# Four graph layers on one core: shorter factor chains in layer 1's preparation, and layer 3's normalisation, weights, products and first row of sums in one block

## Chip, cores and metric

One core of a Trainium2 chip runs the whole program in one launch. The metric is the device time in microseconds (us), and less is better. TensorE is PE in the profile, VectorE is DVE, ScalarE is ACT, GpSimd is POOL, SyncE (which issues most DMAs) is SP.

## What is computed

A node matrix x (3327 x 256, float32) passes four layers that share one 0/1 adjacency (about 1% ones, with a diagonal). Each layer takes h = relu(layernorm(x)) and adds its result to x:

```python
h = jnp.maximum(_layernorm(x), 0.0); x = x + L0(h)   # 8-head graph attention
h = jnp.maximum(_layernorm(x), 0.0); x = x + L1(h)   # cosine attention
h = jnp.maximum(_layernorm(x), 0.0); x = x + L2(h)   # 8-head hard attention (argmax)
h = jnp.maximum(_layernorm(x), 0.0); x = x + L3(h)   # mean over neighbours

# L1:  Wh = h @ W.T;  sim = Wh @ Wh.T / (|Wh| |Wh|.T + EPS);  softmax(masked sim) @ Wh
# L3:  agg = mask @ h / max(deg, 1)
#      out = relu(concat([h @ W_self + b_self, agg @ W_nb + b_nb]) @ W_comb + b_comb)
```

## The kernel before

The nodes are 26 tiles of 128; x stays in SBUF as `k.X`. The layers are separate, with a barrier of all engines between blocks and layers. Within a block each engine has its own list of instructions, written out by hand and taken strictly in order, and semaphores are the only link between the lists. Every float32 operand of a product is split into a float16 high part and a float16 rest; a product is three matmuls per half of the 256 features (`hi_lo_products`), so 6 matmuls of 256 columns per tile.

**Layer 1's preparation** (`cosine_prepare`, L980) handles tiles in four portions (0 to 3, 4 to 11, 12 to 19, 20 to 25) and seven quads of four tiles (the last has two). DVE measures mean and variance (`measure`, L1076, then `gather`, L1081) and finds from them, with a square root on ACT (`root`, L1198) and one Newton step, each tile's factor and shift (`factors`, seven small DVE instructions, L1092 to L1104, each waiting for the one before). POOL applies them (`shifted`, L1035, tile by tile), PE turns the quad by transposes (`turn`, L1278), ACT takes relu and the high part (`high`, L1204), DVE the rest (`low`, L1111). PE multiplies by the weights (`project`, L1292), ACT stores the product Wf and its squared norms (`take`, L1209, L1215), POOL casts (`cast`, L1040) and DVE takes the rest (`rest`, L1117). From the norms in four portions DVE finds 1/|Wh| (`norms`, L1125 to L1138, seven small instructions with a root on ACT, L1221), POOL scales the rows (`unit`, L1047), PE turns them (`unit_turn`, L1309), ACT and DVE split them (`unit_high` L1232, `unit_low` L1144). `row` writes the reciprocal norms to DRAM. The order of each list is written at its end: POOL's runs from `shifted(0)` over `cast(0)`, `shifted(3)`, `shifted(4)`, `cast(1)`, `shifted(5)`, `shifted(6)`, `unit(0)`, `unit(1)`, `cast(2)` on. The attention block `cosine_attend` starts after a barrier.

**Layer 3** has two blocks. The first is `normalise` (L71) with `mean_weights` (L2235) hooked into it: ACT applies factor, shift and relu tile by tile (L190), PE turns quads (L228), ACT and DVE split into `hT` (L196, L168); two halves, 0 to 7 and 8 to 25. The hooked part loads W_self, W_nb, W_comb and the biases, waits for all the loads together, transposes the weights (L2287), multiplies each with W_comb (L2294) and finds the joint bias (L2302, L2280), so that one product per source is left. The second block, `mean_aggregate`, loads the adjacency (two tile rows per transfer) and computes, for all 26 tiles, P = hT @ m, stored as high part and rest side by side (512 columns, L2371, L2406, L2417); then for each of 26 rows of tiles the sum of 26 matmuls of 512 columns (`sums`, L2385) and the row's own product (`own`, 6 matmuls, L2392). Row 0's sums are woven into the products:

```python
for jt in range(NT):
    if i == 0:
        if jt + LEAD < NT:
            neighbour(jt + LEAD)
        pe.wait_ge(s_pl, jt + 1)
```

ACT and DVE finish each row (L2411 to L2429) and SP stores it.

## Time and profile before

| | us |
|---|---|
| median of 3 runs (lowest to highest) | 2209.24 (2208.99 to 2215.06) |
| the profiled execution's own time | 2210.15 |
| its span | 2208.4 |

| engine | busy, us | share of the span |
|---|---|---|
| PE | 1979.8 | 90% |
| DVE | 1877.9 | 85% |
| ACT | 1607.4 | 73% |
| POOL | 914.7 | 41% |

The span goes from the first to the last instruction; 1.75 us of the execution's own time lie around it. The shares are averages over four layers with different limits, and each of the two places changed is a small part of the span. Layer 1's preparation runs from 672.2 to 736.3 us of the span, layer 3's first block from 1983.4 to 2019.3, its second from there to the end. A matmul's record is longer than its turn in the pipeline: back to back, the chain gives 0.216 us for one of 512 columns at full clock.

### The profile page before, as it was taken

To read this page: it belongs to the slowest core of one execution; us is meant where nothing else is said; L and a number is where in the kernel's file an instruction comes from. 1 tells how busy PE (TensorE), PEld (TensorE's weight loads), DVE (VectorE), ACT (ScalarE), POOL (GpSimd) and SP (SyncE) were. 2 spreads that over 40 slices of the span, in tenths; PEclk is the share of its full clock that TensorE was granted. 3 is DMA by queue.
4 is the path that set the end of the run, shared out by engine and by line. 5 is a ranking of instruction groups with operands and counts; after the bars stand their busy time and mean duration, and the time that the engine had idled before them with its cause. 6 is when DMAs were issued, how large, how long until landed. Compare 5 with 4: busy or idle time off the path is not lost. (4 is left out here: it accounts for less than half of the span.)

```text
span 2208.4 us, 58755 instructions
## 1 busy us (share of the span) xinstructions
PE 1979.8 (90%) x23674; PEld 1552.3 (70%) x23674; DVE 1877.9 (85%) x4155; ACT 1607.4 (73%) x1914; POOL 914.7 (41%) x952
## 2 busy tenths in 40 slices
PE   4748999999995899999887999999999999977999
PEld 4548999999994788888654666666666666655544
DVE  5587999999997899988668999999999999985222
ACT  4557999999994776552266999999999999885100
POOL 0020000000005434446316888888888888860000
PEclk9958999999998899999898999999999999997999
DMA  9798221221201156679564212222122211101222
GB/s 306 288 367 308 75 90 57 75 89 55 95 22 41 54 147 160 156 164 190 124 177 144 71 38 69 71 71 70 37 71 71 71 65 42 40 7 48 81 81 71
DMA packets 178078, 235.13 MB, mean 106 GB/s; under 512 B 112195, under 2 KB 143971, under 8 KB 174481
## 3 DMA queue, kind: packets, MB, share of 16 engines
q1 hardware_dynamic: 153408, 203.68, 30.1%
q10 hardware_dynamic: 24400, 27.70, 3.8%
q8 instruction: 188, 3.08, 0.6%
q14 instruction: 82, 0.67, 0.1%
HBM read 161.79 MB, written 49.00 MB: 95 GB/s over the span
## 5 line engine op out<-in xcount | busy, mean ns | idle before, releaser
L2200 DVE CUSTOM_DVE_ANT_0 h_S<-h_ps,off 128x832 f32<-128x832 f32 x832 | 800.1, 1019 | 17.4 <-PE h_ps L2099 16.3
L2099 PE MATMUL h_ps<-KS,QS 98*128 98x416 f16 x1664 | 441.5, 347 | 74.4 <-DVE h_mx L2200 43.0
L2159 ACT ACTIVATE h_H<-h_S,h_nmx 128x2048 fp8e4<-128x2048 f32 x208 | 416.7, 2003 | 69.7 <-DVE h_nmx L2206 69.7
L844 ACT ACTIVATE b_CA<-room,HC 128x1152 fp8e4<-128x1152 f32 (+1 forms) x384 | 435.5, 1219 | 0.0
L945 PE MATMUL b_pb<-xb,room 128*128 128x132 f16 x5408 | 415.8, 222 | 3.6 <-DVE room L906 3.2
L945 PEld LDWEIGHTS b_pb<-xb,room 128*128 128x128 fp8e4 x5408 | 341.9, 97 | 6.5 <-DVE room L906 6.0
L2053 POOL TENSOR_SCALAR h_gap<-h_S,h_nmx 128x1280 f32<-128x1280 f32 x208 | 277.1, 1332 | 91.2 <-DVE h_nmx L2206 81.6
L2058 POOL TENSOR_SCALAR h_H<-h_gap 128x1280 uint8<-128x1280 f32 x208 | 260.5, 1253 | 17.2
L926 PE MATMUL b_pz<-xb,adjT 128*128 128x134 f16 x2704 | 258.1, 222 | 4.3 <-PEq L306 4.3
L2130 PEld LDWEIGHTS h_po<-Vhl,h_HT 128*128 128x128 fp8e4 x5408 | 214.8, 98 | 64.9 <-ACT h_HT L2166 0.7
L2099 PEld LDWEIGHTS h_ps<-KS,QS 98*128 98x128 f16 x1664 | 95.8, 97 | 192.9 <-DVE h_mx L2200 119.0
L1422 POOL TENSOR_SCALAR c_MK<-c_ad 128x512 f16<-128x512 uint8 x169 | 155.1, 917 | 178.7 <-DVE c_V L1523 142.3
L1035 POOL TENSOR_SCALAR p_H<-X,p_sm 128x256 f32<-128x256 f32 x26 | 14.1, 556 | 515.9 <-DVE p_sm L1104 515.8
L2130 PE MATMUL h_po<-Vhl,h_HT 128*128 128x64 f16 x5408 | 225.9, 193 | 0.6 <-ACT h_HT L2168 0.6
L2166 ACT ACTIVATE h_HT<-h_pT 128x1024 uint16<-128x1024 uint16 x208 | 209.3, 1006 | 0.2 <-PE h_pT L2107 0.2
L859 DVE TENSOR_SCALAR b_CD<-room,HC 128x1152 uint8<-128x1152 f32 (+1 forms) x240 | 189.3, 789 | 0.8 <-PEq L306 0.8
L926 PEld LDWEIGHTS b_pz<-xb,adjT 128*128 128x128 fp8e4 x2704 | 184.5, 97 | 4.6 <-issue 4.6
L1579 PE MATMUL c_pa<-WHhi,c_V 128*128 128x257 f16 x676 | 185.6, 275 | 0.6 <-DVE c_V L1523 0.5
L1581 PE MATMUL c_pa<-WHhi,c_V 128*128 128x257 f16 x676 | 184.7, 273 | 0.0
L1580 PE MATMUL c_pa<-WHlo,c_V 128*128 128x256 f16 x676 | 183.9, 272 | 0.0
L906 DVE TENSOR_TENSOR room<-b_CA,adjT 128x288 int32<-128x288 int32 (+1 forms) x384 | 162.4, 442 | 16.0 <-ACT b_CA L844 15.8
L2385 PE MATMUL m_pa<-m_P,m_ad 128*128 128x512 f16 x676 | 154.3, 380 | 0.3 <-DVE m_P L2417 0.3
(246 smaller groups left out, 3192.0 us busy)
## 6 DMA issues: line engine op xcount, KB each, us to landing
h_rows<-in_adj_dram SPq DMA_DIRECT2D x24, 1663.5 KB, 7.4
room<-in_adj_dram SPq DMA_DIRECT2D x25, 832.0 KB, 6.6
room<-in_adj_dram SPq DMA_DIRECT2D x25, 831.5 KB, 7.5
e_dram<-c_U ACTq DMA_DIRECT2D x78, 256.0 KB, 3.1
xb<-xv_dram SPq DMA_DIRECT2D x44, 435.5 KB, 5.1
adjT_dram<-adjT SPq DMA_DIRECT2D x1, 10816.0 KB, 32.2
c_ad<-adjT_dram SPq DMA_DIRECT2D x13, 832.0 KB, 6.8
m_ad<-adjT_dram SPq DMA_DIRECT2D x13, 832.0 KB, 4.5
```

The source lines that it names most:

```text
L844: nc.scalar.activation(dst[:, 0:cols], elr[:, n % 2, 0:cols], ACT.Sigmoid, bias=HC[:, h, 1, jt:jt + 1], scale=STEP, saturate=False).then_i ...
L859: nc.vector.tensor_scalar(dst[:, 0:gn * P].bitcast(U8), elr[:, n % 2, 0:gn * P], HC[:, h, 0, jt:jt + 1], float(FP8_ONE), ALU.is_gt, ALU.mu ...
L926: last = nc.tensor.matmul(pz[:, z % 2, r * WZ:(r + 1) * WZ].rearrange("p (h d) -> p h d", h=2), k.adjT[:, g0 + 3 * b + r, jt, :], xb[:, m ...
L945: last = nc.tensor.matmul(pb[:, p, b, r * W:(r + 1) * W].rearrange("p (f d) -> p f d", f=2), B[:, u % RING_B, t * P:(t + 1) * P], xb[:, m ...
L1579: nc.tensor.matmul(pa[:, q, t, 0:D + 1], hi, WHhi[:, jt, :], start=first, stop=False, skip_group_check=True)
L2053: nc.gpsimd.tensor_scalar(gap[:], S[:, g % 2, CA:NP], nmx[:, g % 2:g % 2 + 1], -SHARPER, ALU.add, ALU.mult).then_inc(s_gap, 1)
L2058: nc.gpsimd.tensor_scalar(H[:, g % 2, CA:NP].bitcast(U8), gap[:], float(FP8_ONE), 0.0, ALU.min, ALU.max).then_inc(s_hB, 1)
L2099: last = nc.tensor.matmul(ps[:, ch % 2, b, 0:SB], QS[:, i % 2, h, :], KS[:, h, c0:c0 + SB], start=True, stop=True)
L2130: last = nc.tensor.matmul(po[:, i % 2, h * 2 * HD:(h + 1) * 2 * HD], wt[:, b, :, e], Vhl[:, b, e, h, :], start=(b == 0 and e == 0), stop=( ...
L2159: nc.scalar.activation(H[:, g % 2, 0:CA], S[:, g % 2, 0:CA], ACT.Exp, bias=nmx[:, g % 2:g % 2 + 1], scale=1.0, saturate=False).then_inc(s_ ...
L2166: nc.scalar.activation(HT[:, g % 2, 0:CA].bitcast(U16), pT[:, 0, :].bitcast(U16), ACT.Copy).then_inc(s_evA, 1)
L2200: nc.vector.tensor_tensor_reduce(out=two(S[:, g % 2, ch * SW:(ch + 1) * SW]), in0=ps[:, ch % 2, :, 0:SB], in1=two(off[:, i % 2, ch * SW:(c ...
```

## The change

**Layer 1's preparation.** The chain of `factors` has five instructions behind ACT's root in place of six, and `norms` five in all in place of seven (the constants move into scalar_tensor_tensor, and the factor 1e-8 moves into ACT's copy of `row`; the attention's logarithm reads the other array accordingly). ACT, not POOL, applies factor and shift to tiles 2, 3, 6, 7, 10 and 11. In DVE's and ACT's lists some entries trade places. In pieces:

```diff
+    COUNTED, NORMED = 7, 6
+    BY_ACT = (2, 3, 6, 7, 10, 11)
     NW = 3
     with ExitStack() as c:
...
             def unit(g):
                 for t in quad(g):
-                    pool.wait_ge(s_rsm, COUNTED * (norm_of(t) + 1))
+                    pool.wait_ge(s_rsm, NORMED * (norm_of(t) + 1))
...
                     elif n == 3:
-                        ins = nc.vector.tensor_tensor(b, a, ve, ALU.mult)
+                        ins = nc.vector.scalar_tensor_tensor(b, a, -0.5 * HSC, ve, ALU.mult, ALU.mult)
                     elif n == 4:
-                        ins = nc.vector.tensor_scalar(a, b, -0.5 * HSC, 1.5 * HSC, ALU.mult, ALU.add)
-                    elif n == 5:
-                        ins = nc.vector.tensor_tensor(rt, a, rs, ALU.mult)
+                        ins = nc.vector.scalar_tensor_tensor(rt, b, 1.5 * HSC, rs, ALU.add, ALU.mult)
                     else:
...
                 nc.vector.reciprocal(inv, root).then_inc(s_rsm, 1)
 
                 dve.wait_ge(s_rsm, at + 3)
-                nc.vector.tensor_tensor(e, inv, low2, ALU.mult).then_inc(s_rsm, 1)
+                nc.vector.tensor_tensor(e, inv, inv, ALU.mult).then_inc(s_rsm, 1)
                 dve.wait_ge(s_rsm, at + 4)
-                nc.vector.tensor_tensor(e, e, inv, ALU.mult).then_inc(s_rsm, 1)
+                nc.vector.scalar_tensor_tensor(e, e, -0.5, low2, ALU.mult, ALU.mult).then_inc(s_rsm, 1)
                 dve.wait_ge(s_rsm, at + 5)
-                nc.vector.tensor_scalar(e, e, -0.5, 1.5, ALU.mult, ALU.add).then_inc(s_rsm, 1)
-                dve.wait_ge(s_rsm, at + 6)
-                nc.vector.tensor_tensor(rcol[:, 0, t0:t1], e, inv, ALU.mult).then_inc(s_rsm, 1)
-                dve.wait_ge(s_rsm, at + 7)
-                nc.vector.tensor_scalar(rcol[:, 1, t0:t1], rcol[:, 0, t0:t1], NORM_EPS, None, ALU.mult).then_inc(s_rsm, 1)
+                nc.vector.scalar_tensor_tensor(rcol[:, t0:t1], e, 1.5, inv, ALU.add, ALU.mult).then_inc(s_rsm, 1)
 
             def unit_low(g):
...
-            measure(4, 6)
+            measure(4, 8)
             factors(0, 1, COUNTED - 1)
-            measure(6, 12)
+            measure(8, 12)
             gather(1)
             factors(1, 0, 1)
             factors(1, 1, COUNTED - 1)
+            measure(12, 14)
             low(0)
-            measure(12, 18)
-            low(1)
-            measure(18, 20)
+            measure(14, 20)
             gather(2)
             factors(2, 0, 1)
-            low(2)
+            low(1)
             factors(2, 1, COUNTED - 1)
             measure(20, NT)
             gather(3)
-            factors(3, 0, COUNTED - 1)
+            factors(3, 0, 1)
+            low(2)
+            factors(3, 1, COUNTED - 1)
             norms(0)
...
-            def take(g):
+            def shifted(t):
+                act.wait_ge(s_sm, COUNTED * (portion_of(t) + 1))
+                nc.scalar.activation(H[:, t, :], k.X[:, t, :], ACT.Identity, scale=rt[:, t:t + 1], bias=nb[:, t:t + 1]).then_inc(s_ha, 1)
+
+            def take(g, part=None):
                 for m in quad_pairs(g):
+                    if part is not None and m % 2:
+                        root(part)
...
             def row(part):
                 t0, t1 = NORM_PORTIONS[part]
                 act.wait_ge(s_row, part + 1)
-                nc.scalar.activation(rT[0:t1 - t0, part, :], pr[0:t1 - t0, 0:P], ACT.Copy).then_inc(s_rowc, 1)
+                nc.scalar.activation(rT[0:t1 - t0, part, :], pr[0:t1 - t0, 0:P], ACT.Copy, scale=NORM_EPS).then_inc(s_rowc, 1)
...
             root(0)
+            shifted(2)
+            shifted(3)
             act.wait_ge(s_wt, 1)
             nc.scalar.activation(w[:, 0], pr[:].rearrange("p (k n) -> p k n", k=KC), ACT.Copy, scale=WSC).then_inc(s_whi, 1)
             root(1)
             high(0)
+            for t in BY_ACT[2:]:
+                shifted(t)
             high(1)
+            root(2)
             take(0)
-            root(2)
             high(2)
-            take(1)
-            root(3)
+            take(1, part=3)
             norm_root(0)
             high(3)
...
         def _(pe):
             def turn(g):
-                pe.wait_ge(s_h, quad(g)[-1] + 1)
+                pe.wait_ge(s_h, sum(t not in BY_ACT for t in range(quad(g)[-1] + 1)))
+                if quad(g)[-1] in BY_ACT:
+                    pe.wait_ge(s_ha, BY_ACT.index(quad(g)[-1]) + 1)
                 for kc in range(KC):
...
-                pe.wait_ge(s_rsm, COUNTED * part + 7)
+                pe.wait_ge(s_rsm, NORMED * (part + 1))
...
+                                               scale=rcol[:, 2 * jp + j:2 * jp + j + 1])
                 ins.then_inc(s_ln, 1)
 
```

**Layer 3.** `normalise` and `mean_weights` give way to one function, `mean_prepare`, with the scheme of layer 1's preparation; `measure`, `gather`, `factors`, `low`, `root`, `high`, `shifted` and `turn` are as there. Its block also makes all the products P (two tiles at a time) and row 0's sums. The weights of the neighbours are loaded, turned and combined first, and each load has its own wait; the first two adjacency loads are issued in this block. `mean_aggregate` starts with `own(0)` and `sums(1)`; its tensors `Pn`, `pa` and `ad` are now made in `layer3`. The final loops over rows are unchanged.

```diff
+def mean_prepare(k, ap, hT, m, bias, ideg, Pn, pa, ad, s_in, s_first, adjT_dram):
...
+    SOURCES_IN = (1, 0)
...
+        @block.sync
+        def _(sp):
+            for s in SOURCES_IN:
+                sp.dma_start(raw[:, s], srcs[s][0].rearrange("(k p) c -> p k c", p=P)).then_inc(s_raw[s], 16)
+            sp.dma_start(comb[:].rearrange("p s k c -> p (s k) c"),
+                         ap["L3_gnn_W_comb"].rearrange("(k p) c -> p k c", p=P)).then_inc(s_comb, 16)
+            for s in range(2):
+                for kc in range(KC):
+                    sp.dma_start(bcol[:, s, kc:kc + 1], srcs[s][1][kc * P:(kc + 1) * P].rearrange("(p o) -> p o", o=1)).then_inc(s_small, 16)
+            sp.dma_start(bc[:], ap["L3_gnn_b_comb"].unsqueeze(0).to_broadcast([P, D])).then_inc(s_small, 16)
+            for q in range(2):
+                sp.dma_start(ad[:, q].rearrange("p t j i -> p t (j i)").bitcast(U8),
+                             adjT_dram[q * CT:(q + 1) * CT].rearrange("t p n -> p t n").bitcast(U8)).then_inc(s_in[q], 16)
...
+            for t in [t for t in range(NT) if t not in BY_ACT]:
+                pool.wait_ge(s_sm, COUNTED * (portion_of(t) + 1))
+                nc.gpsimd.tensor_scalar(H[:, t, :], k.X[:, t, :], rt[:, t:t + 1], nb[:, t:t + 1], ALU.mult, ALU.add).then_inc(s_h, 1)
...
+            def neighbour_low(g):
+                for n in quad_pairs(g):
+                    dve.wait_ge(s_ph, n + 1)
+                    nc.vector.scalar_tensor_tensor(Pn[:, 2 * n:2 * n + 2, D:2 * D], pp[:, n % RP, :].rearrange("p (t d) -> p t d", t=2),
+                                                   AGSC / PSC, Pn[:, 2 * n:2 * n + 2, 0:D], ALU.mult, ALU.subtract).then_inc(s_pl, 1)
...
+            measure(0, 4)
+            gather(0)
+            factors(0, 0, 1)
+            measure(4, 8)
+            factors(0, 1, COUNTED - 1)
+            measure(8, 12)
+            gather(1)
+            factors(1, 0, 1)
+            measure(12, 14)
+            factors(1, 1, COUNTED - 1)
+            measure(14, 20)
+            gather(2)
+            factors(2, 0, 1)
+            weights_low(0)
+            low(0)
+            factors(2, 1, COUNTED - 1)
+            measure(20, 23)
+            low(1)
+            weights_low(1)
+            measure(23, NT)
+            gather(3)
+            factors(3, 0, 1)
+            neighbour_low(0)
+            low(2)
+            factors(3, 1, COUNTED - 1)
+            neighbour_low(1)
+            low(3)
+            dve.wait_ge(s_small, 16 * SMALL)
+            nc.vector.tensor_copy(bb[:], bcol[:].unsqueeze(3).to_broadcast([P, 2, KC, P])).then_inc(s_bb, 1)
+            neighbour_low(2)
+            low(4)
+            neighbour_low(3)
+            low(5)
+            dve.wait_ge(s_b, 1)
+            nc.vector.tensor_tensor(bias[:], pm[:, 0:D], bc[:], ALU.add)
+            neighbour_low(4)
+            low(6)
+            neighbour_low(5)
+            nc.vector.tensor_scalar(dg[:, 0, :], k.deg[:], 1.0, None, ALU.max).then_inc(s_deg, 1)
+            dve.wait_ge(s_deg, 1)
+            nc.vector.reciprocal(dg[:, 1, :], dg[:, 0, :]).then_inc(s_deg, 1)
+            neighbour_low(6)
+            dve.wait_ge(s_deg, 2)
+            nc.vector.tensor_scalar(ideg[:], dg[:, 1, :], 1.0 / AGSC, None, ALU.mult)
...
+            root(0)
+            shifted(2)
+            shifted(3)
+            for n, s in enumerate(SOURCES_IN):
+                act.wait_ge(s_tr, n + 1)
+                nc.scalar.activation(wt[:, s].rearrange("p k n -> p (k n)"), pp[:, n, :], ACT.Copy).then_inc(s_cp, 1)
+            root(1)
+            high(0)
+            for t in BY_ACT[2:]:
+                shifted(t)
+            weights_high(0)
+            root(2)
+            high(1)
+            weights_high(1)
+            neighbour_high(0)
+            high(2)
+            root(3)
+            neighbour_high(1)
+            for g in range(3, QUADS):
+                high(g)
+                neighbour_high(g - 1)
+            neighbour_high(QUADS - 1)
...
+            def neighbour(g):
+                pe.wait_ge(s_lo, KC * (g + 1))
+                for n in quad_pairs(g):
+                    if n >= RP:
+                        pe.wait_ge(s_pl, n - RP + 1)
+                    for e in range(2):
+                        t = 2 * n + e
+                        for x, (kc, a, b) in enumerate(prods):
+                            last = nc.tensor.matmul(pp[:, n % RP, e * D:(e + 1) * D], hT[:, a, kc, t * P:(t + 1) * P], m[:, b, 1, kc, :],
+                                                    start=(x == 0), stop=(x == len(prods) - 1), skip_group_check=True)
+                    last.then_inc(s_p, 1)
+
+            def first_sums(g):
+                if g == 0:
+                    pe.wait_ge(s_in[0], 16)
+                for n in quad_pairs(g):
+                    pe.wait_ge(s_pl, n + 1)
+                    for jt in (2 * n, 2 * n + 1):
+                        last = nc.tensor.matmul(pa[:, 0, :], ad[:, 0, 0, jt, :], Pn[:, jt, :], start=(jt == 0), stop=(jt == NT - 1))
+                if g == QUADS - 1:
+                    last.then_inc(s_first, 1)
...
+            def combine(n):
+                s = SOURCES_IN[n]
+                pe.wait_ge(s_cp, n + 1)
+                if n == 0:
+                    pe.wait_ge(s_comb, 16)
+                else:
+                    pe.wait_ge(s_mlo, n)
...
+            turn(0)
+            combine(0)
+            turn(1)
+            combine(1)
+            for g in range(QUADS):
+                if 1 <= g < QUADS - 1:
+                    turn(g + 1)
+                neighbour(g)
+                if g == 3:
+                    pe.wait_ge(s_bb, 1)
+                    pe.wait_ge(s_mlo, 2)
+                    for n, (s, kc) in enumerate([(s, kc) for s in range(2) for kc in range(KC)]):
+                        last = nc.tensor.matmul(pm[:, 0:D], bb[:, s, kc, :], comb[:, s, kc, :], start=(n == 0), stop=(n == 2 * KC - 1))
+                    last.then_inc(s_b, 1)
+                if g >= 2:
+                    first_sums(g - 2)
+            first_sums(QUADS - 2)
+            first_sums(QUADS - 1)
...
+        def summed(eng, i):
+            eng.wait_ge(*((s_agg, i) if i else (s_first, 1)))
...
-                if c >= 2:
-                    sp.wait_ge(s_agg, CT * (c - 1))
+                sp.wait_ge(s_agg, CT * (c - 1) - 1)
...
-            for t in range(LEAD):
-                neighbour(t)
-            for i in range(NT):
+            own(0)
+            for i in range(1, NT):
                 sums(i)
                 own(i)
...
-        normalise(k, "n3", hT, [], also=lambda c1: mean_weights(k, c1, ap, m, bias, ideg))
-        mean_aggregate(k, hT, m, bias, ideg, adjT_dram, out_dram)
-
-
+        Pn = k.sb(c, "m3_P", [P, NT, 2 * D], F16)
+        ad = k.sb(c, "m3_ad", [P, 2, CT, NT, P], FP8)
+        pa = k.ps(c, "m3_pa", [P, 2, CH])
+        s_in = [k.sem(f"s_m3_in{i}") for i in range(2)]
```

## Rows read from the trace of the kernel before

**Rows 1.** The chain that ended last, from the aggregation block's start: start, length, what.

```profile
2019.28 4.80 DMA m_ad<-adjT_dram
...
2044.18 0.66 PE m_pp L2371 x6
2044.83 0.21 PE m_pa L2385
...
2047.03 0.66 PE m_po L2392 x6
2047.68 5.61 PE m_pa L2385 x26
```

**Rows 2.** Windows in layer 3: stretch, length, busy of each engine (instructions), granted clock (PEclk), DMA.

```profile
1983.40:1992.40 9.00, 0.00 (x0) 0.00 (x0) 8.85 (x40) 1.49 (x2) 0.00 (x0) 0.50 0.49 134
...
2004.00:2010.00 6.00, 3.94 (x16) 3.14 (x16) 2.58 (x4) 6.00 (x13) 0.00 (x0) 0.50 0.00 0
...
2024.00:2027.30 3.30, 3.17 (x14) 2.09 (x15) 0.42 (x1) 0.38 (x1) 0.00 (x0) 0.50 0.36 144
2027.30:2047.00 19.70, 19.41 (x153) 14.71 (x152) 9.35 (x22) 8.43 (x22) 0.00 (x0) 1.00 0.00 1
```

**Rows 3.** Timeline of layer 3's two blocks: start, length, engine, line, what, count [idle before].

```profile
1983.43 0.40 SPq L2256 DMA_DIRECT2D w_raw<-in_L_gnn_W_self_dram  x1
...
1984.13 2.71 DVE L149 BATCH_NORM_STATS2 n_stats<-X 128x6 f32<-128x256 f32 x8
...
1992.50 1.97 PE L2287 MATMUL w_pt<-ident,w_raw 128*128 128x128 f32 x8 [12.71 <-DMA w_bc<-in_L_gnn_b_comb_dram]
...
1994.30 4.88 PE L2294 MATMUL w_pm<-w_comb,w_t 128*128 128x256 f32 x16
...
1995.00 4.03 ACT L190 ACTIVATE n_h<-X,n_sm 128x256 f32<-128x256 f32 x8
...
2016.00 2.48 PE L2302 MATMUL w_pt<-w_comb,w_bb 128*128 128x256 f32 x8
...
2017.41 1.28 DVE L2277 SCALAR_TENSOR_TENSOR m_w<-w_pm,m_w 128x512 f16<-128x512 f32 x2
2018.61 0.41 DVE L2280 TENSOR_TENSOR m_bias<-w_pt,w_bc 128x256 f32<-128x256 f32 x1
```

**Rows 4.** Timeline of the cosine preparation, first two thirds.

```profile
677.75 0.63 DVE L1081 BATCH_NORM_AGGREGATE p_mv<-p_stats 128x2 f32<-128x6 f32 x8
...
687.78 1.04 PE L1278 MATMUL p_pt<-ident,p_H 128*128 128x128 f32 x8
...
689.19 0.22 ACT L1198 ACTIVATE p_sm<-p_sm 128x8 f32<-128x8 f32 x1
...
692.17 0.17 DVE L1104 SCALAR_TENSOR_TENSOR p_sm<-p_mv,p_sm 128x8 f32<-128x8 f32 x1
...
692.44 4.31 POOL L1035 TENSOR_SCALAR p_H<-X,p_sm 128x256 f32<-128x256 f32 x8 [3.16 <-DVE p_sm L1104]
...
701.32 5.47 POOL L1047 TENSOR_SCALAR p_H<-p_Wf,rcol 128x256 f32<-128x256 f32 x8
...
709.44 0.58 DVE L1125 TENSOR_SCALAR p_rs<-p_n 128x8 f32<-128x8 f32 x1
...
711.35 0.17 DVE L1138 TENSOR_SCALAR rcol<-rcol 128x8 f32<-128x8 f32 x1
```

**Rows 5.** Two lines of the cosine preparation: count, ns min/median/max, first and last start.

```profile
L1047 POOL TENSOR_SCALAR p_H<-p_Wf,rcol x26: 472/478/1477, 701.3 to 728.3; 128x256 f32<-128x256 f32 x26
L1117 DVE TENSOR_TENSOR WHlo<-p_Wf,WHhi x13: 678/871/1099, 701.0 to 728.8; 128x512 f16<-128x512 f32 x13
```

**Rows 6.** Timeline of the cosine preparation, end, and the next block's first matmuls.

```profile
728.46 1.94 PE L1309 MATMUL p_pn<-ident,p_H 128*128 128x128 f32 x8 [4.23 <-DVE WnT L1144]
...
735.54 0.42 DVE L1144 TENSOR_TENSOR WnT<-p_pn,WnT 128x256 f16<-128x256 f32 x1 [0.37 <-ACT WnT L1232]
...
736.29 12.72 PE L1563 MATMUL c_pd<-WnT 128*128 128x256 f16 x96 [1.20 <-PEq L991]
```

241 lines of the change are left out of this document (133 added, 108 removed).

## The prediction, on record before the changed kernel ran

> **What bounds the kernel at the two places.** I read the chain that ended last first. From 2047.03 on it is PE alone: 6 matmuls for a row's own product (0.66) and 26 for its sums (5.61, so 0.216 each), 25 times over, at full clock. The change leaves this stretch alone, so layer 3 can gain only what lies between its start at 1983.43 and 2047.03 [rows 1, 3]: 63.6 us. The windows show what PE does in them: nothing for 9 us, then transposes at the lower level of its clock (0.50, that is 1.2 GHz) with gaps in which it waits for ACT, busy throughout; after the block change it idles again on the adjacency load, and only from 2027.3 runs full at 1.00 (2.4 GHz) [rows 1, 2]. PE does not limit the first 40 us; the order of the work does. One wait for eight loads, released at 1992.50, holds the weights [rows 3].
>
> In layer 1's preparation (672.2 to 736.3) nothing is full. The timeline is read for what keeps POOL from starting: its third batch waits 3.16 us for a factor chain on DVE that ended at 692.34, and that chain waited for the root on ACT at 689.19, which stands behind `take(0)` in ACT's list. From 692.44 POOL runs without a gap until it hands over casts to DVE, and DVE reaches `norms(1)` at 709.44 [rows 4]. The end is a relay of PE, ACT and DVE: 728.46 to 736.29 [rows 6].
>
> **Layer 3, step by step.** Times are from the block's start (1983.43 = 0). Unit costs: a measurement 0.33 (8 in 2.71, overlapped), a gather 0.08 (8 in 0.63), a small factor instruction 0.17 and with its semaphore 0.2, a tile shifted on POOL 0.54 (8 in 4.31) or ACT 0.50 (8 in 4.03), a 512-column split on DVE 0.65 (2 in 1.28), 8 transposes 1.04 at the higher level and 1.94 at the lower, 4 float32 combining matmuls 2.44 (half of 4.88) [rows 3, 4, 6].
>
> 1. Four measurements, four gathers, epsilon: 1.9. Four more measurements stand ahead of the reciprocal: 3.2. Five chain instructions: 4.2. Two tiles each, POOL and ACT side by side: 5.3. The two weight loads are now the first on SP, 0.4 per issue; an 832 KB load took 4.8 [rows 1, 3], so even that price puts the second, smaller one at 5.7. I take no cost and keep 0.5.
> 2. `turn(0)` at the lower level to 7.3, `combine(0)` to 9.8.
> 3. Meanwhile DVE: 4 measurements, 8 gathers, epsilon, 2 measurements, chain: 7.9. Then 6 measurements, 8 gathers, epsilon: 10.7. ACT shifts four tiles from 8.0 to 10.1 and takes the weights' high part to 10.7. DVE: their rest to 11.4, then `low(0)`, which frees the first half of PE's bank at 12.05. Here PE idles for 2.2.
> 4. `turn(1)` at the lower level and paced by `low(0)` to 13.6, `combine(1)` to 16.0.
> 5. From 16.0 PE has work without a gap: 26 products at 0.655, 17.0; 36 transposes, 4.7; the bias product, 2.5; 26 sums, 5.6. Sum 29.8, end at 45.8. When PE started at 2024.0 it was at the lower level until 2027.3 [rows 2]; here it starts at 12.05, so it should be up by 16.
> 6. Block change 0.3 (DVE's last at 2019.02, SP's load at 2019.28; also 735.96 to 736.29) plus 0.2 for the last matmul's end [rows 1, 3, 6]: `own(0)` at 46.3 in place of 63.6. Gain 17.3.
>
> What hides the rest: beside step 5 DVE has about 22 us (13 pairs of product rests and 12 splits at 0.65, 6 measurements, two chains, 2 us of odds), ACT about 14, POOL 14 tiles, 7.6. Were that cover gone, the first thing late would be `low(2)`, which I get at 21.6, against `turn(3)`, due at 22.1; later quads have 2 us or more. SP's list grows: ten issues in a row (two weights, W_comb, four bias columns, a bias row, two adjacency loads), 4 us at 0.4 each, so the first adjacency tile lands near 9 and is needed at 25; before, it was issued at 2019.28 and PE stood until it landed, which is inside the 17.3 [rows 1]. The load for rows 4 and 5 still waits for row 1's sums, with two more rows (12.5 us) to land in. The widening of the pair instructions saves ACT and DVE time that limits nothing. ScalarE's new operation (Identity with two operands from memory) is in neither block; the nearest row is relu of the same shape, 0.50. If it were 0.1 slower, four tiles would cost 0.4.
>
> Bounds: 18.5, if steps 2 to 4 run partly at the higher level and the gaps close; 15, if PE is at the lower level for two more quads' worth of work (2.5). I take 17.
>
> **Layer 1's preparation.** `root(2)` moves ahead of `take(0)`, DVE's `low(1)` ahead of the chain, `low(0)` behind two measurements. With the unit costs above, from the block's start at 672.2: the first chain ends at 676.4 (two measurements later, one instruction earlier than before), the first quad, shared with ACT, is ready at 677.5, the second chain ends at 680.0. Two measurements to 680.65, `low(0)` to 681.9, six measurements, eight gathers and epsilon to 684.7, ACT's root beside `low(1)` to 685.95, five chain instructions: the third chain ends at 686.9 instead of 692.34. PE turns quad 1 from 681.35, when the first half of `low(0)` is done, and projects quad 0 by 686.6. POOL is then still in `cast(0)`, whose second pair waits for ACT's Wf (687.3, then 0.6 for the cast), until 687.9. So POOL's long run starts at 687.9 instead of 692.44: 4.5. The run has the same parts in the same order, and nothing else gates it: the fourth chain is done near 692 and needed at 693.5, the first norms near 693.3 and needed at 697.
>
> `norms` loses two instructions of 0.2 in each portion. After `norms(1)` (seven in 2.1, from 709.44 to 711.52) DVE gates `low(5)` and `unit_low(0)`; the next two gate POOL's `unit` and the relay's first `unit_low`: 3 x 0.4 = 1.2 at most, 0.7 taken, as ACT's root stands in the middle of each. The relay at the end stays. Sum 5.2.
>
> How long the run is depends on one thing. Eight `unit` tiles took 5.47, though the median is 0.478; one took 1.477, and the DVE line `rest` beside it stretches from 0.68 to 1.10 [rows 4, 5]. In the new order `rest(0)` and `rest(1)` fall beside the shifts instead; if collisions go away, 8 x 0.478 = 3.8 and 1.6 more are gained (6.8); if they move along, 5.2 stands. I take 6. The Trainium skill (SBUF — State Buffer, "Who interferes with whom") speaks for the second: a VectorE instruction with two SBUF inputs and a GpSimd instruction that reads SBUF exclude each other for the whole of one instruction, whichever kind of GpSimd work it is. By that rule alone the gain would be 5.2; the 1.477 (0.478 and about one `rest`) agrees with it.
>
> The small chain instructions beside POOL are exposed to the same thing; one of them took 0.58 in place of 0.17 at 709.44 [rows 4], so each could lose 0.4. Bounds: 8 above; below 3, if two chains are stretched so on the path.
>
> **Sum.** The profiled execution took 2210.15, 1.75 beyond its span and 0.9 above the median of 2209.24. 2210.15 - 17 - 6 = 2187.2 for such an execution, 2186.2 for the median. The forecast's own range is 15 to 18.5 and 4.5 to 8: 2182.7 to 2189.7. I count 0.3% (6.6 us) as what a measurement of this kernel can tell from no change.
>
> **Rivals.**
> - *A new round trip in layer 3.* Each quad goes PE, ACT, DVE, PE. If ACT's and DVE's strict order (split of a quad behind product parts of the one before) makes PE wait, a quad costs a turn 1.04, two ACT and two DVE splits, about 2.4, and the products 2.6, in series with the sums 0.9: 6.9 against 4.6. Over three of the quads that is 7: gain 10, total 2193. For it: the 0.5 us margin at `turn(3)`. Against: the turn stands ahead of the previous quad's products. 0.14.
> - *Layer 1's preparation gives nothing,* since another wait takes over before `norms(1)` or PE's relay starts from the last squared norms on ACT: 17 alone, 2192. Against it: the relay's wait of 4.23 us at PE names DVE [rows 6], and DVE's two late `norms` are in that path. 0.15.
> - *Slower: PE stays at the lower level through the merged block.* It did so from 2004 to 2010, two thirds busy [rows 2]. Then step 5's 29.8 become about 59.6, steps 3 and 4 take 1 more, and `own(0)` comes at 77 against 63.6: 13.5 lost, less 3 to 6 in layer 1, 2217 to 2220. With layer 1 gaining 3 it is slower by over 0.3% once nine tenths of step 5 are low (29.8 x 0.9 - 17.3 - 3 = 6.5); at half of it layer 3 still gains 2. Against: with work at hand PE went to 1.00 after 3.3 us and stayed [rows 2]. 0.03.
> - *It does not do what it says:* PE's work is only moved, and what it saves in front comes back as gaps between the finer waits, in both places. Gain 0 to 6, 2203 to 2209. 0.04.
>
> The forecast keeps 0.64. The range reaches over the first two rivals and 1.7 below the forecast's own: 2181 to 2196. Faster takes the forecast and two rivals, 0.93; same 0.04; slower 0.03.
>
> **What would show it.** In the new profile: the first product near 16 after the block's start; PE at 1.00 and over 95% busy from there to the block's end; `own(0)` near 46; then rows of 6.27 as before. In layer 1: POOL's batch of tiles 12 to 19 at 688, `norms(1)` near 704, the attention's first matmul near 730. A clock of 0.50 after 16 us, or PE waiting for DVE splits in every quad, would make the prediction wrong; so would an attention start within 2 us of 736.

## The result, and the profile after

The changed kernel took 2190.22 us (median of 4 runs, 2186.02 to 2191.85) against 2209.11 (4 runs, 2208.65 to 2215.06): ratio 0.9898, 95% interval 0.9886 to 0.9911. Measured twice more, on two chips, it took 2187.71 and 2187.61 against 2212.70 and 2213.19, ratios 0.9882 [0.9867, 0.9897] and 0.9876 [0.9859, 0.9894]. The forecast was 2186.2, range 2181 to 2196.

| us of the profiled execution | before | after |
|---|---|---|
| its own time, its span | 2210.15, 2208.4 | 2191.85, 2190.1 |
| layer 0 and what stands ahead of layer 1 (not touched) | 672.2 | 675.1 |
| layer 1's preparation | 64.1 | 58.7 |
| cosine attention, layer 2's preparation, hard attention (not touched, but for one operand's name) | 348.5, 83.9, 814.7 | 348.7, 85.7, 815.5 |
| layer 3, start to `own(0)` | 63.44 | 44.89 |
| from there to the end | 161.6 | 161.6 |

`own(0)` is row 0's own product; its first matmul is recorded at 2046.87 before (the chain of [rows 1], which the prediction used, has 2047.03) and at 2028.56 after. The two changed stages gained 5.4 and 18.6, together 24.0, where the forecast said 6 and 17. Over the whole kernel PE was busy for 1977.4 us (90%), against 1979.8. The stages that were not touched were 5.7 us longer, and the runs below are what tells whether that comes with the change.

Layer 3 from its start to `own(0)`, before and after (length, then busy of PE, PE's weight loads, DVE, ACT and POOL with the number of instructions, granted clock, DMA):

```profile
1983.43:2046.87 63.44, 44.25 (x267) 34.49 (x268) 33.88 (x113) 33.12 (x73) 0.00 (x0) 0.76 0.15 47
```

```profile
1983.67:2028.56 44.89, 38.88 (x267) 32.04 (x268) 33.64 (x110) 22.07 (x43) 11.02 (x20) 0.87 0.21 66
```

PE's idle time fell from 19.2 to 6.0 us. That is 13.2 of the 18.6. The other 5.4 is the same number of matmuls done in less time: PE was busy for 38.88 in place of 44.25, at a mean granted clock of 0.87 in place of 0.76.

Layer 3, PE in the timeline of the changed kernel (start, length, engine, line, what, count, idle before and what ended it). The block starts at 1983.67, so 16 us after it is 1999.67:

```profile
1986.58 1.97 PE L2486 MATMUL p_pp<-ident,w_raw 128*128 128x128 f32 x8 [6.55 <-DMA w_raw<-in_L_gnn_W_nb_dram]
1989.05 1.96 PE L2457 MATMUL p_pt<-ident,p_H 128*128 128x128 f32 x8 [0.50 <-POOL p_H L2298]
1990.81 2.47 PE L2498 MATMUL p_pm<-w_comb,w_t 128*128 128x256 f32 x8
1995.56 1.94 PE L2457 MATMUL p_pt<-ident,p_H 128*128 128x128 f32 x8 [2.28 <-DVE hT L2337]
1997.29 2.64 PE L2498 MATMUL p_pm<-w_comb,w_t 128*128 128x256 f32 x8
1999.77 2.78 PE L2468 MATMUL p_pp<-m_w,hT 128*128 128x256 f16 x24
2002.39 1.04 PE L2457 MATMUL p_pt<-ident,p_H 128*128 128x128 f32 x8
2003.26 2.78 PE L2468 MATMUL p_pp<-m_w,hT 128*128 128x256 f16 x24
...
2013.73 1.89 PE L2514 MATMUL p_pm<-w_comb,w_bb 128*128 128x256 f32 x8
2015.46 1.03 PE L2478 MATMUL m_pa<-m_P,m_ad 128*128 128x512 f16 x4
...
2025.91 2.32 PE L2478 MATMUL m_pa<-m_P,m_ad 128*128 128x512 f16 x10
2028.56 0.81 PE L2576 MATMUL m_po<-m_w,hT 128*128 128x256 f16 x6 [0.32 <-PEq L2260]
```

Against [rows 3]: the weights are turned 2.9 us after the block's start in place of 9.1, the first quad stands at 5.4, and the one long stop that is left, 2.28, waits for DVE's first split. Two windows of the same kernel, up to the first product and from there to the last sum (columns as above):

```profile
1995.56:1999.77 4.21, 4.21 (x17) 3.70 (x18) 3.40 (x11) 1.20 (x2) 2.75 (x6) 0.62 0.14 54
1999.77:2028.26 28.49, 28.46 (x227) 23.17 (x225) 18.77 (x44) 13.25 (x25) 4.99 (x9) 1.00 0.01 1
```

From the first product to the last sum PE is busy for 28.46 of 28.49 us at full clock. DVE beside it has 18.8, ACT 13.3. In the old layer 3 PE was full at 1.00 only from 2027.3 on [rows 2].

Layer 1's preparation in the changed kernel (start 675.11), DVE and POOL:

```profile
687.28 1.28 DVE L1112 SCALAR_TENSOR_TENSOR p_hT<-p_pt,p_hT 128x512 f16<-128x512 f32 x2
688.48 0.19 DVE L1097 RECIPROCAL p_sm<-p_sm 128x8 f32<-128x8 f32 x1
...
689.31 0.51 DVE L1105 SCALAR_TENSOR_TENSOR p_sm<-p_mv,p_sm 128x8 f32<-128x8 f32 x1
...
690.50 0.62 POOL L1043 TENSOR_SCALAR WHhi<-p_Wf 128x512 f16<-128x512 f32 x1 [0.68 <-ACT p_Wf L1213]
...
691.10 4.34 POOL L1038 TENSOR_SCALAR p_H<-X,p_sm 128x256 f32<-128x256 f32 x8
...
694.95 1.68 DVE L1105 SCALAR_TENSOR_TENSOR p_sm<-p_mv,p_sm 128x6 f32<-128x6 f32 x1
...
696.74 4.75 POOL L1038 TENSOR_SCALAR p_H<-X,p_sm 128x256 f32<-128x256 f32 x6
...
701.47 4.09 POOL L1050 TENSOR_SCALAR p_H<-p_Wf,rcol 128x256 f32<-128x256 f32 x8
...
706.19 2.85 DVE L1118 TENSOR_TENSOR WHlo<-p_Wf,WHhi 128x512 f16<-128x512 f32 x2 [2.97 <-POOL WHhi L1043]
708.96 0.16 DVE L1126 TENSOR_SCALAR p_rs<-p_n 128x8 f32<-128x8 f32 x1
...
733.80 1.44 PE L1572 MATMUL c_pd<-WnT 128*128 128x256 f16 x6 [1.20 <-PEq L992]
```

The third chain no longer holds POOL: it starts its tiles 12 to 19 right behind a cast that waited for ACT's product, 15.99 us into the stage against 20.26 before. The run behind is no shorter than before, though: the eight scaled tiles fell from 5.47 to 4.09, and the six shifts ahead of them rose from 3.30 to 4.75. A factor instruction of 0.17 took 1.68 beside POOL: it started at 694.95 and ended at 696.63, as POOL's two casts did.

### The profile page after: what moved, and what is told of

Its sections match the earlier page's. It is cut to its first block and busy times, and to the rows that moved or that the text cites. A ratio compares the mean times of both kernels' runs of the same rounds, so it can differ in the third digit from the quotient of the medians.

```text
span 2190.1 us, 58736 instructions
## 1 busy us (share of the span) xinstructions
PE 1977.4 (90%) x23674; PEld 1550.2 (71%) x23674; DVE 1877.1 (86%) x4140; ACT 1599.8 (73%) x1889; POOL 924.1 (42%) x966
## 5 line engine op out<-in xcount | busy, mean ns | idle before, releaser
L2177 ACT ACTIVATE h_HT<-h_pT 128x640 uint16<-128x640 uint16 x208 | 145.2, 698 | 0.0
```

## The experiments

Each profiled execution was cut into stages by the first instruction of each (layer 1's preparation: its first instruction to the attention's; layer 3: first load to `own(0)`), since the untouched stages scatter by more than the effects looked for. Five kernels were run once, for their traces alone, and their times say nothing on effects of this size: `cos_order_act` 2208.98, `l3_split_waits` 2210.16, `l3_more_dve` 2187.78, `long_norms` 2191.29, `no_act_l1` 2189.71. Over all profiled executions here layer 0 took 672.2 to 676.2 us, layer 2's preparation 83.3 to 86.0, hard attention 814.2 to 815.5, with one code each (but for one chain edited in `best`).

**The whole change again, and each half alone.** First run: the changed kernel once more. The two halves: the kernel before with the new layer 3 alone, and with the new layer 1 alone.

`only_l3` against the kernel before, then `only_cos` against the changed kernel (the functions called are as in the one and the other):

```diff
-        normalise(k, "n3", hT, [], also=lambda c1: mean_weights(k, c1, ap, m, bias, ideg))
-        mean_aggregate(k, hT, m, bias, ideg, adjT_dram, out_dram)
+        mean_prepare(k, ap, hT, m, bias, ideg, Pn, pa, ad, s_in, s_first, adjT_dram)
+        mean_aggregate(k, hT, m, bias, ideg, Pn, pa, ad, s_in, s_first, adjT_dram, out_dram)
```

```diff
-        mean_prepare(k, ap, hT, m, bias, ideg, Pn, pa, ad, s_in, s_first, adjT_dram)
-        mean_aggregate(k, hT, m, bias, ideg, Pn, pa, ad, s_in, s_first, adjT_dram, out_dram)
+        normalise(k, "n3", hT, [], also=lambda c1: mean_weights(k, c1, ap, m, bias, ideg))
+        mean_aggregate(k, hT, m, bias, ideg, adjT_dram, out_dram)
```

> The changed kernel once more, nothing edited. Its first profile lost 18.3 us against before, though the two places changed lost 5.4 (layer 1's preparation, 64.1 to 58.7) and 18.6 (layer 3 up to its first own product, 63.6 to 45.0): layer 0 was 2.9 us longer (672.2 to 675.1) and the stretch from layer 2's start to layer 3's 2.5 us longer (898.7 to 901.2), both in code that the change does not touch. Theory A (these two are variation from execution to execution): the new profile shows other lengths there, and the timed executions spread over some 5 us with a median between 2185 and 2191. Theory B (they come with the change, by its effect on what follows): again 675 and 901 within 0.5, and a median of 2190. Both: 58.7 and 45.0 again within 0.3.

> Layer 3's half of the change alone; layer 1's preparation as before. Its own effect by the first profile is -18.6. Theory A: median near 2209 - 18.6 = 2190.5, less or more by the same variation of layers 0 and 2. Theory B with the loss tied to layer 1's edit (its earlier end or its other layout of memory): layer 0 at 672 and layer 2 at 898.7, so 2190.5 and thus the same as the whole change. Layer 1's preparation 64.1 in both.

> Layer 1's half alone; layer 3 as before. Theory A: preparation 58.7, median near 2203.7 (-5.4), with the same spread of layers 0 and 2. Theory B tied to layer 1's edit: the preparation still 58.7, but layers 0 and 2 longer by 5 together, so a median near 2209 and no gain.

Measured on one chip, the kernel before 2212.70 (2208.93 to 2219.95, 20 runs):

| kernel | median us | ratio, 95% interval | layer 1's preparation | layer 3 to `own(0)` |
|---|---|---|---|---|
| before (profile of the first measurement) | 2212.70 | | 64.1 | 63.4 |
| again | 2187.71 | 0.9882 [0.9867, 0.9897] | 58.6 | 43.4 |
| only_l3 | 2191.89 | 0.9910 [0.9894, 0.9925] | 65.4 | 44.8 |
| only_cos | 2207.57 | 0.9974 [0.9962, 0.9985] | 58.7 | 64.3 |

The gains of the halves, 20.8 and 5.1, add to 25.9 against 25.0 for both: no interaction is seen beyond the intervals, some 3 us each. The stretches outside the two stages wander either way (layer 0 took 676.2 us with the new layer 3 alone, its own code as before, in the longest of that kernel's six executions, 2199.66), so the 18.9 of the first medians and the 25 here are taken for one effect seen through that scatter. Their intervals overlap, and what makes those stages vary is not shown. What the change itself is worth is read from the stages: 23.9 to 25.5 in the three profiled executions of the changed kernel, against the first profile of the kernel before.

**The shorter chains alone, and the order and ACT's share alone.**

Both against the kernel before, in layer 1 alone: `cos_chain` has the short `factors` and `norms` with every list as it was, `cos_order_act` the new lists and `BY_ACT` with the long ones.

```diff
-    COUNTED = 8
+    COUNTED, NORMED = 7, 6
...
-                        ins = nc.vector.tensor_tensor(b, a, ve, ALU.mult)
+                        ins = nc.vector.scalar_tensor_tensor(b, a, -0.5 * HSC, ve, ALU.mult, ALU.mult)
...
```

```diff
     COUNTED = 8
+    BY_ACT = (2, 3, 6, 7, 10, 11)
...
+            measure(12, 14)
             low(0)
-            measure(12, 18)
-            low(1)
-            measure(18, 20)
+            measure(14, 20)
...
```

> Of layer 1's half only the shorter chains (factors five for six behind the root, norms five for seven in all); order of the lists and POOL's share as before. The prediction gave 0.7 to the chains and at most 1.2. The two profiles give 2.0 behind norms(1): 0.83, 0.41 and 0.76 at the three places where DVE gates. Theory C (the three add in full, and the batch start of POOL gains up to one instruction, 0.2, twice): the preparation shortens by 2.0 to 2.6, to about 61.8. Theory D (most of the 2.0 came from the new order, by other collisions with POOL): by 0.7 to 1.2, to about 63.1.

> Layer 1's preparation alone, with the new order of the lists and ACT's share of the shifts, but the factor chains of seven and the norms of seven instructions. The preparation took 64.1 and 65.4 us with the old code in the two profiled executions, 58.6 to 58.7 with all of the change (three executions), and 61.4 with the shorter chains alone. If the two parts add (theory: each is a term of its own on the path), the order and ACT's share are worth what is left: 2.5 to 3.4 us, a preparation of 61 to 62 us. If the order only pays once the chains are short (rival: each portion's long chain holds POOL's run as before), it stays above 63 us. If the order carries the whole gain and the chains only overlap with it, it falls below 60 us. The one time is no evidence, since the unchanged layers vary by 3 us between executions; the stretch in the trace is read.

`cos_chain` 2210.02, ratio 0.9986 [0.9975, 0.9996], preparation 61.4; `cos_order_act` preparation 60.6. Against 64.1 that is 2.6 and 3.5, the sum 6.1, and the whole 5.4 to 5.5: nearly additive, though 60.6 lies 0.4 below the range expected. Such differences are good to about half a us: the old stage took 63.7, 64.1 and 65.4 in three executions, the changed one 58.3 to 59.2 in seven. Cut at the first instruction of `norms(1)`:

| us | start to `norms(1)` | `norms(1)` to the attention's first matmul |
|---|---|---|
| before | 37.26 | 26.85 |
| cos_chain | 36.22 | 25.25 |
| cos_order_act | 33.80 | 26.86 |
| changed (first profile; again) | 33.85; 33.91 | 24.84; 24.71 |
| the same code of layer 1 in `l3_fill`; `best` (below) | 33.18; 33.12 | 25.16; 25.37 |

The order brings 3.5, all of it ahead of `norms(1)`. The chains bring 1.0 there in the old order, and in the new one nothing by the first profile or 0.6 to 0.7 by the last row; behind `norms(1)` they bring 1.6 in the old order and 1.5 to 2.1 in the new, where the forecast had 0.7. Why one code has two rows is the next experiment's subject. (The left column scatters more than the right: the old stage took 38.40 in the profile of `only_l3`, and its first 24 product matmuls ran at a lower clock, 4.71 us against 3.57.)

**The long norms put back.**

```diff
-    COUNTED, NORMED = 7, 6
+    COUNTED, NORMED = 7, 8
...
-                nc.vector.tensor_tensor(e, inv, inv, ALU.mult).then_inc(s_rsm, 1)
+                nc.vector.tensor_tensor(e, inv, low2, ALU.mult).then_inc(s_rsm, 1)
                 dve.wait_ge(s_rsm, at + 4)
-                nc.vector.scalar_tensor_tensor(e, e, -0.5, low2, ALU.mult, ALU.mult).then_inc(s_rsm, 1)
+                nc.vector.tensor_tensor(e, e, inv, ALU.mult).then_inc(s_rsm, 1)
                 dve.wait_ge(s_rsm, at + 5)
-                nc.vector.scalar_tensor_tensor(rcol[:, t0:t1], e, 1.5, inv, ALU.add, ALU.mult).then_inc(s_rsm, 1)
+                nc.vector.tensor_scalar(e, e, -0.5, 1.5, ALU.mult, ALU.add).then_inc(s_rsm, 1)
+                dve.wait_ge(s_rsm, at + 6)
+                nc.vector.tensor_tensor(rcol[:, t0:t1], e, inv, ALU.mult).then_inc(s_rsm, 1)
+                dve.wait_ge(s_rsm, at + 7)
+                nc.vector.tensor_scalar(scaled[:, t0:t1], rcol[:, t0:t1], NORM_EPS, None, ALU.mult).then_inc(s_rsm, 1)
```

> The changed kernel, with layer 1's norms in their old form (seven instructions on DVE in each of the four portions instead of five; POOL and PE wait for all of them). The prediction took 0.7 us for all portions together, at most 1.2. Theory now: each of the three later portions stands in full on the path and its small instructions are stretched beside POOL, so the preparation takes 1.5 to 2.2 us more than the changed kernel's 58.6, 60.1 to 60.8. Rival (the prediction's size): 59.2 to 59.8, and the rest of the 2.0 us gained behind norms(1) comes from other things moving.

The preparation took 59.9, between the two sizes expected. Behind `norms(1)` it needed 26.95, the old 26.85. Ahead of it this kernel was 0.9 faster than the changed one, 32.98. POOL in this kernel, to be held against the rows above:

```profile
696.48 3.23 POOL L1039 TENSOR_SCALAR p_H<-X,p_sm 128x256 f32<-128x256 f32 x6
699.69 5.46 POOL L1051 TENSOR_SCALAR p_H<-p_Wf,rcol 128x256 f32<-128x256 f32 x8
705.12 3.23 POOL L1044 TENSOR_SCALAR WHhi<-p_Wf 128x512 f16<-128x512 f32 x4
```

The same instructions as in the changed kernel took 3.23, 5.46 and 3.23 in place of 4.75, 4.09 and 2.38. DVE ahead of `norms(1)` here, the first instruction of `norms(1)`, and POOL behind the chain's end:

```profile
705.77 2.10 DVE L1119 TENSOR_TENSOR WHlo<-p_Wf,WHhi 128x512 f16<-128x512 f32 x2 [2.04 <-POOL WHhi L1044]
...
707.80 0.58 DVE L1127 TENSOR_SCALAR p_rs<-p_n 128x8 f32<-128x8 f32 x1
...
709.98 2.30 POOL L1051 TENSOR_SCALAR p_H<-p_Wf,rcol 128x256 f32<-128x256 f32 x5 [1.62 <-DVE p_scaled L1140]
```

The rest took 2.10 where the changed kernel's took 2.85, which is where 0.75 of the 0.9 comes from. From `norms(1)` to POOL's scaling it is 2.18 here (707.80 to 709.98) and 1.34 in the changed kernel: two instructions of 0.2 less, and 0.42 less for the first one, stretched beside POOL's cast here and not there.

This second difference isn't the two instructions' doing. `l3_fill` and `best` (below) have the changed kernel's layer 1 line for line, and their casts, rests and first instruction look like this kernel's. In `best`:

```profile
704.74 3.24 POOL L1043 TENSOR_SCALAR WHhi<-p_Wf 128x512 f16<-128x512 f32 x4
705.39 2.10 DVE L1118 TENSOR_TENSOR WHlo<-p_Wf,WHhi 128x512 f16<-128x512 f32 x2 [2.97 <-POOL WHhi L1043]
707.42 0.58 DVE L1126 TENSOR_SCALAR p_rs<-p_n 128x8 f32<-128x8 f32 x1
```

So there are two patterns at this place. In one, POOL's last two casts and DVE's two rests take 1.05 and 1.09 each, and the first instruction of `norms(1)` 0.58; so it was in `l3_fill`, `best`, `long_norms` and all five profiles in which the old order or the long chains stand. In the other the four casts take 0.62 each, DVE's first rest stands until they are over (2.25) and the first instruction then takes 0.16; so it was in the six others (`no_act_l1`, below, among them), all with the new order and the short norms. The first pattern reaches `norms(1)` some 0.7 earlier and takes 0.4 more behind it. Why the same code falls into one or the other isn't shown. Compared within the first pattern, the norms' two instructions a portion are worth 1.6 behind `norms(1)`: the three portions there take 1.99, 1.58 and 2.86 in `long_norms` and 1.59, 1.17 and 2.09 in `best`. On the whole preparation it is 59.9 against 58.3 and 58.5, 1.4 to 1.6. That is the low end of the first theory and above the rival.

**All tiles back on POOL in layer 1.**

```diff
-    BY_ACT = (2, 3, 6, 7, 10, 11)
+    BY_ACT = ()
...
             root(0)
-            shifted(2)
-            shifted(3)
```

> The changed kernel, with all 26 tiles of layer 1's preparation shifted by POOL again (order of DVE's and ACT's lists and the short chains as in the changed kernel). Theory: ACT's share is worth the shorter first quad (two tiles beside two instead of four in a row, 1.1 us), which goes in full down the path to POOL's long run; the four tiles of the second portion fall before POOL's wait for ACT's first product and cost nothing. So the preparation takes 59.5 to 60.0 us against 58.6. Rival 1: POOL's four further tiles come on top, 3.2 us more in all (61.8). Rival 2: ACT's share is worth nothing, since another thing gates POOL's run, within 0.3 us of 58.6.

59.3 us, a little under the theory's range, and 0.1 to 1.0 above the seven executions with the changed stage (58.3 to 59.2, five of them 58.4 to 58.7). The first quad's four tiles took 2.17 in a row in place of 1.10; POOL's tiles 12 to 19 began at 16.8 in place of 15.9 to 16.4. So ACT's share is worth 0.4 to 0.9 at the start of POOL's run. That POOL's four further tiles come on top is refuted; between the theory's size and nothing at the stage's end the scatter leaves it open.

**Separate waits in the old layer 3.** Each weight load and W_comb get a semaphore of their own; the rest of the old block stays.

```diff
-        pe.wait_ge(s_in, 16 * LOADS)
         for s in range(2):
+            pe.wait_ge(s_raw[s], 16)
...
+        pe.wait_ge(s_comb, 16)
```

> The kernel before, with one thing of the change: in layer 3's first block the two weight loads, W_comb and the biases have waits of their own instead of one wait for all eight. PE's transposes of the weights then start about 3 us after the block's start instead of 9.1. Theory: the first 40 us were bound by the order of the work over PE, ACT and DVE, and of the 19 to 20 us that the whole rewrite gained, the joint wait is a small part: it brings PE's first quad forward by 2.3 us (the quad's tiles come from ACT, whose chain stays), so own(0) comes 2 to 3 us earlier, 61 us after the start instead of 63.5 to 64.3. Rival 1: the joint wait was all of the head of the block; 5 to 6 us earlier. Rival 2: ACT's tile by tile work bounds the block anyway; within 1 us of before.

`own(0)` came 61.0 us after the block's start; with the old block it came at 63.0 to 64.3 in four executions, 63.4 in the first profile, so 2 to 3 us earlier. PE in this kernel (block's start 1985.82):

```profile
1988.46 1.11 PE L2288 MATMUL w_pt<-ident,w_raw 128*128 128x128 f32 x4 [6.29 <-DMA w_raw<-in_L_gnn_W_self_dram]
...
1993.06 5.61 PE L2296 MATMUL w_pm<-w_comb,w_t 128*128 128x256 f32 x16 [1.70 <-DMA w_comb<-in_L_gnn_W_comb_dram]
1998.51 1.91 PE L228 MATMUL n_pt<-ident,n_h 128*128 128x128 f32 x16
2003.85 1.97 PE L228 MATMUL n_pt<-ident,n_h 128*128 128x128 f32 x8 [3.44 <-ACT n_h L190]
...
2024.04 1.33 PE L2373 MATMUL m_pp<-m_w,hT 128*128 128x256 f16 x6 [2.83 <-DMA m_ad<-adjT_dram]
```

The transposes of the weights start 2.6 us into the block in place of 9.1 [rows 3], and PE's stop moved to the load of W_comb, then to ACT's tiles and to the adjacency as before. The joint wait, the most striking row of the old block, was some 2.4 of the 18.6 to 20 us that the rewrite brought. The rest was not taken apart by runs: the rows before show ACT's tiles (a stop of 3.44 and smaller ones) and the adjacency load (2.83), and both are gone in the changed kernel, but what the sharing of the tiles by POOL and ACT, the merged block and the early adjacency loads are worth each is not shown.

**Some 5 us more for DVE in the new block.** DVE gets 15 further `bn_stats` instructions (the ones that `measure` consists of), whose results are not used; all other work stays.

```diff
                                                    ALU.max, ALU.subtract).then_inc(s_lo, 1)
+                if g >= 2:
+                    for x in range(3):
+                        nc.vector.bn_stats(spare[:, 4 * g + x, :], k.X[:, x, :])
```

> The changed kernel, with 15 more measurements on DVE (3 behind each of the splits of quads 2 to 6, results not used; 0.33 us each by the old trace, some 5 us in all) in layer 3's new block. Theory: from the first product on PE is the bound and DVE has a cover of some 8 us, so own(0) comes 0 to 1.5 us later than in the changed kernel (43.4 to 44.9 us after the start in three executions), and PE's idle time in the block grows by no more than that. Rival: DVE's strict order is nearly on the path already, and own(0) comes 3 to 5 us later, at 47 to 50 us.

`own(0)` at 43.40, as in `again` (43.39). One window from the first product to the last sum, of this kernel and then of `again`:

```profile
1995.69:2024.18 28.49, 28.46 (x227) 23.17 (x225) 23.58 (x61) 13.25 (x25) 6.29 (x12) 1.00 0.01 1
```

```profile
1995.89:2024.38 28.49, 28.47 (x227) 23.14 (x225) 19.58 (x46) 13.23 (x25) 6.45 (x12) 1.00 0.00 1
```

All 15 fall within that window (61 DVE instructions for 46). DVE's busy time rises from 19.6 to 23.6, and PE's row doesn't move. The stretch is PE's, and the rival of the round trip is out.

**The stop ahead of the second quad filled.** In the changed kernel the second combination of weights comes behind `turn(1)`; here it stands ahead, in another bank of PSUM.

```diff
             turn(0)
             combine(0)
-            turn(1)
             combine(1)
+            turn(1)
+            pe.wait_ge(s_mlo, 1)
```

> The changed kernel, with the second combination of weights (of the layer's own source) made ahead of the second quad's transposes and into another PSUM bank, and its high part taken by ACT ahead of the second quad's. In the changed kernel PE stands for 2.3 us ahead of turn(1), waiting for DVE's first split, and then makes a combination of 2.6 us before the first product. Theory: that stop is filled, so everything behind it comes 2.0 to 2.5 us earlier: own(0) at 41.5 to 42.8 us after the block's start against 43.4 to 44.9, ratio to the kernel before about 0.987, which is 1 to 2 us below the changed kernel. Rival: the stop only moves (ACT and DVE reach turn(1)'s quad later, since the second combination's parts now stand ahead in their lists), and own(0) stays at 43.4 or later.

2185.56 (2184.42 to 2185.81), ratio 0.9877 [0.9861, 0.9894]; `own(0)` at 42.4. It gained 1.0 against `again`, whose PE had nearly the same clock there, not the 2.0 expected: the first product came 1.7 earlier (12.9 us after the start, for 14.6), and 0.6 of it came back at a stop ahead of the fourth product pair.

```profile
1991.82 1.16 PE L2458 MATMUL p_pt<-ident,p_H 128*128 128x128 f32 x8 [0.82 <-DVE hT L2338]
1992.82 2.78 PE L2471 MATMUL p_pp<-m_w,hT 128*128 128x256 f16 x24
1995.44 1.04 PE L2458 MATMUL p_pt<-ident,p_H 128*128 128x128 f32 x8
1996.31 1.47 PE L2471 MATMUL p_pp<-m_w,hT 128*128 128x256 f16 x12
1998.26 1.48 PE L2471 MATMUL p_pp<-m_w,hT 128*128 128x256 f16 x12 [0.48 <-DVE m_P L2344]
```

**The changed kernel a third time, and a version with that second stop taken away too.** `best` is `l3_fill` with DVE's rests of the first two pairs ahead of its last measurements, and the short factor chain in layer 2's preparation as well.

```diff
+            neighbour_low(0)
             measure(23, NT)
             gather(3)
             factors(3, 0, 1)
-            neighbour_low(0)
             low(2)
```

> The changed kernel once more, to stand beside the next one on the same chip: 2187 to 2190 us, ratio to the kernel before 0.987 to 0.991. Layer 3's block to own(0) takes 43.4 us if PE stays at full clock through turn(1) and the combination behind it, and 44.9 if it falls to half there (both have been seen in profiled executions of this code); nothing else in the block may differ by more than 0.2 us.

> The kernel l3_fill with two more edits: in layer 3's block DVE takes the rests of the first two product pairs ahead of its last three measurements (in l3_fill PE stood there for 0.8 us, waiting for DVE, which gave back part of the filled stop), and layer 2's preparation has the factor chain of five instructions behind the root in place of six. Theory: the stop ahead of the fourth pair goes, own(0) at 41.5 to 42.0 us after layer 3's start (l3_fill 42.4; the changed kernel 43.4 or 44.9); layer 2's preparation gains 0 to 0.8 us, which its own scatter (83.3 to 86.0) can hide. Time 2184 to 2186 us, ratio to the kernel before 0.985 to 0.988, 2 to 3 us below the changed kernel in the same call. Rival: PE's stop moves to turn(3), since DVE's measurements of the last tiles come later, and own(0) stays at 42.4 or more.

`changed_3` 2187.61, ratio 0.9876 [0.9859, 0.9894]; `best` 2187.23, 0.9877 [0.9862, 0.9892]. In `best` the stop ahead of the fourth pair is gone and one ahead of `turn(3)` is there in its place, `own(0)` at 42.37: the rival's outcome. PE in `best`:

```profile
1996.28 2.78 PE L2469 MATMUL p_pp<-m_w,hT 128*128 128x256 f16 x24
1999.47 1.16 PE L2456 MATMUL p_pt<-ident,p_H 128*128 128x128 f32 x8 [0.41 <-DVE hT L2336]
```

DVE worked without a gap from 1992.8 to 1999.8 there. No version was measured faster than the changed kernel by more than the intervals; the 1.0 us of filling is seen in the traces alone. Layer 2's preparation took 84.0 in `best`, inside its scatter, so the short chain there stays undecided.

## Why the prediction was right, step by step

**Sum.** 2186.2 was given as 2209.24 less 23. The median fell by 18.9 in the first measurement and by 25.0 and 25.6 in the two later ones. The stages gained 24.0 in the first profile, where untouched stages were 5.7 longer. The case that was forecast happened; that 2190.22 is 4 from 2186.2 and not closer is that scatter, as far as the profiles show.

**Layer 3, steps 1 to 4** hold to 0.2 in the first profile (forecast in brackets): first quad 5.4 (5.3), first combination 7.1 (7.3), second quad's turn 11.9 (12.05), first product 16.1 (16.0). The loads cost nothing, as taken. The tight place that was named, `low(2)` done at 21.6 and `turn(3)` at 22.1, was at 21.6 and 22.2, and `best` stopped just there. That 16.0 was met to a tenth is partly luck: the sum took the lower clock for PE's part of these steps, and the first product came at 14.6 where the second quad's turn and the second combination ran at full clock (`again`), and at 16.8 in `long_norms`.

**Step 5** was sized 29.8 and took 28.5. Two terms were too big. The 36 transposes were taken at 0.13, a record's length, where eight in a row take 0.87 until the next instruction starts (2002.39 to 2003.26), so 3.9 and not 4.7; the text ahead of the prediction warns of this for the 512-column matmul. The bias product was taken at 2.5 [rows 3], a record at a granted clock of 0.76; at 1.00 its record is 1.89, and it holds PE for 1.73 (2013.73 to 2015.46). So `own(0)` came at 44.9 and not 46.3, and at 43.4 where the clock was better. The gain of 18.6 to 20.0 lies at and above the bound of 18.5 given for this layer: the bound allowed for a better clock in steps 2 to 4, not for a shorter step 5.

**The clock** was foreseen to rise by 16. In the first profile it was mixed until then (0.62 in the last window before the first product) and 1.00 from there on. It differs between executions, as told below.

**Layer 1, the start of POOL's run**: 15.99 (15.7 forecast), a gain of 4.3 (4.5). The cause named, that the third chain gates POOL and the cast behind ACT's product comes next, is what the rows show. ACT's share in it is 0.4 to 0.9 by `no_act_l1`.

**Collisions**: they moved along. The run took 0.1 us more than before, and the 1.6 that I allowed for their going away wasn't there; the taken 6 should have been 5.2 at this step. The skill's rule (the Trainium skill, SBUF — State Buffer, "Who interferes with whom"), that a DVE instruction with two SBUF inputs and POOL's reading lock each other out for a whole instruction, spoke for that; by it the gain would be 5.2, and the trace agrees: 1.45 more on the shifts, 1.38 less on the scaling. In all 14 profiles the six shifts and eight scalings together took 8.7 to 8.9, whichever of the two was the longer (3.2 to 5.1 and 3.7 to 5.5). What the trace shows beyond one instruction at a time: a rest stood until three casts in a row were over (2.25, where alone it takes 0.68), and the factor instruction of 1.68 stood through a shift and two casts. The measured 5.4 agrees with the rule's sum for a partly different reason, next.

**Norms**: taken 0.7, at most 1.2; measured 1.6 within one pattern of collisions, and 2.0 in the first profile. Behind `norms(1)` five executions with the long form took 26.73 to 27.04, and eight with the short one and the new order 24.70 to 25.37. The term mis-sized is "0.7 taken, as ACT's root stands in the middle of each": the root's place doesn't hide anything, since POOL's scaling starts only when the chain is over (in `long_norms` its row waits for the last instruction of it), and the removed instructions aren't 0.2 each when POOL is running. By portion the shortening is 0.4, 0.4 and 0.8; in the last the two that went had taken 0.44 and 0.54. The bound was set by the unstretched duration although the stretched row (0.58) was at hand. The other 0.4 of the first profile's 2.0 is that row itself, 0.16 there for 0.58, and it was paid for ahead of `norms(1)`, where DVE's pair of rests took 2.85 for 2.10. So the 5.4 is right partly by luck, misses that cancel: 4.3 (start) less 0.1 (run), less 0.8 (rests and casts ahead of `norms(1)`), plus 2.0.

**Rivals.** A round trip in layer 3: refuted, DVE has at least 4 us to spare in the window and is tight only in its first 7 us, which `l3_fill` and `best` ran into. Layer 1 gives nothing: refuted by `only_cos`. PE at the lower clock through the block: didn't occur in any of the nine executions with the new block, though a small part of it did, ahead of the first product. The work only moved: refuted by both stages.
